# A one-core decoder layer: every second score block of group 0 copied out of PSUM by ScalarE and masked by GpSimd

## What is computed

```python
q = (q @ fq1_w.T + fq1_b) * (q @ fq2_w.T + fq2_b)      # 16 heads of 16 features
k = (k @ fk1_w.T + fk1_b) * (k @ fk2_w.T + fk2_b)
# chunks of 64 tokens: masked scores inside a chunk, a running sum k^T v before it
s = jnp.where(tril, qc @ kc.T, 0.0)
o = inter + s @ vc                                      # linear: no softmax
o = o * rsqrt(mean(o * o, -1) + EPS) * norm_w
x = layernorm(x + o @ wo.T)
```

## Time and profile before

| | us |
| --- | --- |
| median of 3 runs | 573.58 |
| lowest, highest | 573.35, 573.89 |
| the profiled execution | 574.25 |
| its span | 572.5 |
| busy in the span: PE, DVE, ACT, POOL | 531.6, 381.1, 156.8, 132.2 |

### The profile page before, as it was taken

One profiled execution on the slowest core, in us unless ns is written; L12 is line 12 of the kernel. 1 busy time (PEld: TensorE's weight loads), 2 busy tenths in 40 slices (PEclk: granted clock), 3 DMA queues, 4 the chain that ended last, 5 costly groups with the idle time before them and its releaser, 6 DMA issues.

```text
span 572.5 us, 8538 instructions
## 1 busy us (share of the span) xinstructions
PE 531.6 (93%) x3152; PEld 426.0 (74%) x3152; DVE 381.1 (67%) x814; ACT 156.8 (27%) x291; POOL 132.2 (23%) x195
## 2 busy tenths in 40 slices
PE   5975699799999999999999999999999999899994
PEld 5734587646887888765888888765888888688883
DVE  4597589877689976875455666875455677823234
ACT  3433101443323222242222112152222111223330
POOL 2020384110005433121004333121004451200001
PEclk9996699989999999999999999999999999999998
DMA  7423231311114110032001110031002110000001
GB/s 204 126 52 82 74 92 56 97 46 26 37 38 131 43 40 9 1 96 91 1 0 60 37 43 10 0 95 55 1 1 56 47 48 0 32 6 2 1 0 37
DMA packets 25257, 26.80 MB, mean 47 GB/s; under 512 B 2816, under 2 KB 22784, under 8 KB 25216
## 3 DMA queue, kind: packets, MB, share of 16 engines
q1 hardware_dynamic: 14208, 15.73, 9.5%
q10 hardware_dynamic: 10576, 8.95, 5.2%
q0 software_dynamic: 432, 1.57, 0.8%
HBM read 24.15 MB, written 2.10 MB: 46 GB/s over the span
## 4 chain that ended last, share of the span: by engine, by line
PE 79%; DVE 12%; issue 3%; ACT 2%; POOL 1%; DMA 1%; ACTq 0%; POOLq 0%; DVEq 0%
PE bank L955 18%; PE bank L957 17%; PE bank L956 17%; PE bank L1002 5%; PE bank L1065 5%; PE bank L1068 5%; PE bank L1066 5%; PE bank L1042 3%; PE bank L1012 2%; DVE qbd L707 2%; DVE weight L664 1%; PE bank L1076 1%; DMA wo_sb<-in_woT 1%; PE bank L1024 1%; DVE ffn_lo L671 1%
## 5 line engine op out<-in xcount | busy, mean ns | idle before, releaser
L955 PE MATMUL bank<-x2T_lo,ffn_hi 128*128 128x512 f32 x256 | 110.9, 433 | 5.0 <-DVE x2T_lo L833 2.9
L906 DVE TENSOR_TENSOR inter<-bank,inter 128x512 f32<-128x512 f32 x64 | 44.2, 690 | 99.7 <-PE bank L957 99.7
L957 PE MATMUL bank<-x2T_hi,ffn_hi 128*128 128x512 f32 x256 | 102.0, 398 | 0.0
L956 PE MATMUL bank<-x2T_hi,ffn_lo 128*128 128x512 f32 x256 | 101.4, 396 | 0.0
L446 POOL TENSOR_TENSOR qbd<-qT_sb,ctxT_sb 128x256 f32<-128x256 f32 x128 | 79.8, 647 | 85.0 <-PE bank L1068 68.7
L955 PE MATMUL bank<-ffn_lo,inter_hi 128*128 128x256 f32 x256 | 77.8, 304 | 1.3 <-DVE inter_lo L900 1.0
L396 POOL TENSOR_TENSOR ve<-ve,minus_half 128x2 f32<-128x2 f32 x24 | 16.8, 716 | 266.7 <-DVE ve L757 198.3
L605 ACT ACTIVATE inter_hi<-inter 128x512 fp32r<-128x512 f32 x64 | 40.4, 632 | 129.4 <-DVE inter L906 129.4
L957 PE MATMUL bank<-ffn_hi,inter_hi 128*128 128x256 f32 x256 | 72.5, 283 | 0.0
L956 PE MATMUL bank<-ffn_hi,inter_lo 128*128 128x256 f32 x256 | 72.4, 283 | 0.0
L599 ACT ACTIVATE inter<-bank 128x512 f32<-128x512 f32 x64 | 38.1, 595 | 124.9 <-PE bank L957 124.9
(11 more groups left out here) (118 smaller groups left out, 793.8 us busy)
## 6 DMA issues: line engine op xcount, KB each, us to landing
toep_sb<-in_toep ACTq DMA_DIRECT2D x64, 128.0 KB, 2.1
xT_sb<-in_xT SPq DMA_DIRECT2D x4, 512.0 KB, 5.4
ctxT_sb<-in_ctxT SPq DMA_DIRECT2D x4, 512.0 KB, 4.7
x_sb<-in_x SPq DMA_DIRECT2D x4, 512.0 KB, 5.8
ctx_sb<-in_ctx SPq DMA_DIRECT2D x4, 512.0 KB, 6.5
out<-ctxT_sb POOLq DMA_DIRECT2D x3, 512.0 KB, 3.4
raw_w<-in_gate_p SPq DMA_DIRECT2D x8, 128.0 KB, 2.3
raw_s<-in_gate_s SPq DMA_DIRECT2D x8, 128.0 KB
```

The lines of the kernel that those rows point to most:

```text
L906: nc.vector.tensor_tensor(inter[:, n % 2, :], up_ps[:, :], inter[:, n % 2, :], ALU.mult).then_inc(inter_ready, 1)
L955: nc.tensor.matmul(ps, w_hi, x_lo, start=start, stop=False, skip_group_check=True)
L956: nc.tensor.matmul(ps, w_lo, x_hi, start=False, stop=False, skip_group_check=True)
L957: return nc.tensor.matmul(ps, w_hi, x_hi, start=False, stop=stop, skip_group_check=True)
```

## The change

In group 0 the blocks v = 1, 3, 5 and 7 no longer go through DVE. ACT copies each of their two banks into `sc_sb[1]`, and POOL sets the part above the diagonal to zero there with one `affine_select` over 128 x 1024 elements. PE's waits are split to match: the banks of an odd block are free when ACT has copied them, and O(v) of an odd v waits for POOL. In ACT's and POOL's queues the new work stands ahead of the spread of v + 2 that the same call issues (on POOL for odd v; on ACT the spreads belong to even v). Groups 1 to 3 do the same work as before, with the counts of the waits adjusted.

```diff
+        def copied(g, v):
+            return g == 0 and v % 2 == 1 and v < 8
@@ gpsimd: score(g, v)
+                if copied(g, v):
+                    pool.wait_ge(sraw_ready, 2 * (v // 2 + 1))
+                    rows = sc_sb[v % 2].rearrange("p n h c -> p (n h) c")
+                    nc.gpsimd.affine_select(out=rows, in_=rows, compare_op=ALU.is_ge, fill=0.0, base=0,
+                                            pattern=[[0, HT], [1, P]], channel_multiplier=-1)\
+                        .then_inc(sp_ready, 1)
                 if v + 2 < 8 and v % 2:
                     spread(g, v + 2)
@@ scalar: score(g, v)
+                if copied(g, v):
+                    count(act, s_mm, 8, g, v + 1)
+                    count(act, o_mm, 8, g, v - 1)
+                    for r in range(2):
+                        nc.scalar.activation(sc_sb[v % 2][:, r].rearrange("p h c -> p (h c)"),
+                                             score_ps(g, v)[r][:, :], ACT.Copy).then_inc(sraw_ready, 1)
                 if v + 2 < 8 and v % 2 == 0:
                     spread(g, v + 2)
@@ vector: score(g, v)
-                if v == 8:
+                if v == 8 or copied(g, v):
                     return
@@ tensor
+            def masked(g, v):
+                if g == 0 and v % 2:
+                    pe.wait_ge(sp_ready, v // 2 + 1)
+                elif g == 0:
+                    pe.wait_ge(sm_ready, v + 2)
+                else:
+                    count(pe, sm_ready, 16, g, 2 * v - 6)
@@ tensor: score(g, v), before the scores of v
-                    count(pe, sm_ready, 16, g, 2 * (v - 1 if g == 0 else v))
+                    if g:
+                        masked(g, v - 1)
+                    elif v >= 2 and copied(0, v - 2):
+                        pe.wait_ge(sraw_ready, 2 * (v // 2))
+                    elif v >= 2:
+                        masked(0, v - 2)
@@ tensor: score(g, v), before the output of v - 1
-                    count(pe, sm_ready, 16, g, 2 * v + 2)
+                    masked(g, v)
@@ tensor: sums(g, mt)
-                count(pe, sm_ready, 16, g, 14 if g == 0 else 16)
+                masked(g, 6 if g == 0 else 7)
```

More of the change, by code:

```diff
@@ L178, in decoder_layer @@
             "filled", "const_ready", "pool_mask", "kv_ready", "prod_ready")
-        last_mm, last_stored = sems("last_mm", "last_stored")
+        last_mm, last_stored, sraw_ready, sp_ready = sems("last_mm", "last_stored", "sraw_ready", "sp_ready")
         rstd_ready = sems("rstd_ready1", "rstd_ready2", "rstd_ready3")
```

## The result

The changed kernel takes 576.09 us (median of 19 runs, 573.87 to 579.56), the kernel before 573.63 us in the same comparison (19 runs). The ratio is 1.0037 with a 95% interval of 1.0023 to 1.005, so the change costs 1.3 to 2.9 us, 2.1 by the ratio itself. (The two medians lie 2.46 us apart; the verdicts here go by the ratio.) Timed again beside other kernels the ratio was 1.0028, interval 1.0016 to 1.004. The forecast was 575.6, slower by 2.0.

What follows compares the result with a forecast made beforehand. DVE was taken to bound group 0's score stage, 4.47 us for two blocks. A POOL loop of 4.88 us put `sums(1)` 1.84 us later; with 0.2 for contention, 573.58 + 2.0 = 575.6 us, range 574.0 to 578.6.

Steps and rivals of the forecast that it cites:

- What bounds: Group 0's score stage: DVE is full with masks and unpack, 4.47 us for two blocks against PE's 3.26.
- where the shift goes: End of group 0's score stage: the later start of `sums(1)` carries to the kernel's end one for one, +2.0 us.
- the walk: Score stage followed event by event from S0 at 26.67 to `sums(1)` at 47.92 us, 1.84 later than before.
- The loop: Odd blocks: S(v), ACT copies, POOL select, then the spread queued behind it, which S(v + 2) awaits; 4.88 us.
- The select: POOL's select of 128 x 1024 in each odd block, taken as 1.3 us between bounds of 1.03 and 2.35.
- Two of POOL's 0.12: SBUF contention in the score stage: two POOL operations on the path each 0.12 us longer, counted as 0.2 us.
- DVE's 0.85: Score stage: DVE's loss when L671 meets a spread (1.53 for 0.68 us), taken as hidden by 1.6 us slack.
- third rival: Dearer POOL work in the score stage, by element cost or DVE operations coming first; +1.8 to 4.2 us on top, 19%.
- DVE's idle time: Score stage: the 4.8 us taken from DVE become idle time ahead of even masks, some 1 to 2 us a lap.
- first rival's point of decision: DVE relief wins in the score stage if each of four selects is 0.8 us shorter than taken; 6%.
- The clock: PE's granted clock stays 1.00 through the score stage to about 46 us; a fall, up to +2.6 us, had 8%.
- parts named for "slower": Whole kernel: chance of being slower by more than 0.2%, given as 0.72, summed from shares of the forecast and its rivals.

Runs made afterwards that it cites:

- e1: Changed kernel with POOL's spread of v + 2 put ahead of the select of v; ratio to the kernel before 0.9999, stage 19.54 us.
- e4: Changed kernel with the score stage's four weight units moved to group 0's convolution; stage 19.69 us, whole 587.01 us in one run, only the stage is read.
- e2: Changed kernel with the select over one head, 128 x 128, the other seven left unmasked (work left out); ratio to the kernel before 0.9972.
- e5: Kernel before plus a POOL select of 128 x 1024 after the spreads of 3, 5 and 7 that nobody waits for; ratio 1.0069.
- e3: Changed kernel with only block 7 copied by ACT and masked by POOL, blocks 1, 3 and 5 through DVE as before; ratio to the kernel before 0.9984.

## Why the prediction was right, point by point

**What bounds, and where the shift goes.** That the stage was DVE's was right. That the shift of its end carries to the end of the kernel one for one agrees with the ratios and is not shown more closely: `outproj` starts 3.02 us later (57.92 for 54.90), at 205.70 us the shift is 2.27 in one execution and 0.44 in the other, and the forecast had 2.0 at both places. The times of events were close, measured from S0. The forecast column is the walk, without the 0.2 us for contention; with it `sums(1)` stood at 48.1, which is 21.4 from S0.

| | forecast | measured |
| --- | --- | --- |
| S3 | 6.08 | 5.73 |
| S5 | 10.96 | 10.73 |
| S7 | 15.84 | 15.74 |
| O7 | 19.72 | 19.79 |
| `sums(1)` | 21.25 | 21.26 |

**The loop.** The named mechanism, the spread behind the select, is shown by e1: turning these two round takes 1.72 of the stage's 1.85 us away. It is half of the cause: with the queue as it was and the unpack away (e4), 1.57 of them go too. The lap came out at 5.00 for a forecast of 4.88.

**The select was mis-sized, with the right sum.** I took 1.30 us; with nothing in its way it is 1.09, close to the 1.12 that POOL's two-input rows gave and far from 1.75 and 2.35. Beside DVE it is 1.57. Four of them are 1.09 + 3 x 1.57 = 5.80, and I had 5.2 and 0.2 for contention. The difference of 0.4 was more than paid by hops that were shorter than I took them: ACT to POOL 0.07 for 0.15, the spread's end to PE 0.05 for 0.14, PE to ACT 1.18 for 1.23. So errors in both directions met, and it is luck that +1.85 agrees with +2.0 better than the terms do. That the profiled execution, at 576.46, came so close to the forecast's 576.25 is luck as well, since +1.13 and -0.8 us of it come from outside the stage.

**Contention was the failed step.** "Two of POOL's 0.12" stood for it. That figure was one meeting in which POOL had started first, and so hardly waited; DVE's 0.85 was the waiting side. In this loop the select starts 0.07 us behind L687 each time, since both are counted from the end of the same spread: it releases S3 and with it the copy and the select, and it ends DVE's L697 and with it the mask, L680 and L687. So POOL is the one that waits, for what is left of L687. By the Trainium skill (SBUF — State Buffer, Who interferes with whom) the port pair that the two engines share is an exclusive lock, and issue order decides who is blocked. The trace agrees, 1.57 us for 1.09, and e2 and e4 show it: the same 0.48 or 0.49 us on 128 elements as on 1024, and none with the units moved. This was the third rival's mechanism, at 0.48 us in three selects; what I had as 0.68 in each lap. It was the forecast's and the rival's at once, and they should not have been set against each other.

**DVE's idle time did not come.** I expected 1 to 2 us of idle DVE in each lap. The view of busy time shows 4.00 of 4, since the two L697 count as busy while they wait for POOL. In the changed kernel that costs nothing further: O3 waits for the select (0.45 us of idle PE ahead of it), not for mask 2; the 0.77 us that PE waits for mask 2 ahead of O2 are over well before. In e5, where DVE is the bound, the same waiting costs 0.9 us and more a lap.

**The first rival's point of decision** was right in kind. With the select 0.79 us shorter (0.78 for 1.57) e2 is faster than before. So the sign of this change hung on the length of one POOL instruction, as the sum had it. **The clock** held to 1.00 up to 46 us in the changed kernel, as forecast; e5 shows that a wait of 2.83 us in this stage was followed by the lower level.

**What wasn't forecast** is what the surroundings add to a single execution: +1.13 and -0.8 us in the profiled one. The first is the landing of `wo_sb`, long before the stage. It took 6.3 us in the kernel before and 6.9 to 7.95 in the changed kernel and its variants; with one profiled execution of the kernel before it stays open whether the kernel has a part in that. Whether the earlier rise of the clock in `outproj` follows from the later start of the stage stays open: it was 6.13 us before, 5.59 and 5.30 in two executions of the changed kernel, but 6.32 in e1 and 6.67 in e3. The recorded chances hold one small slip: the parts named for "slower" add up to 0.73, not 0.72.

## What to carry to other kernels

When work is moved to an engine with idle time, look first at what stands behind it in that engine's queue and is waited for by another: here 4.8 us taken from the full engine were worth nothing, because a spread that PE needs was put behind a select that it doesn't need yet, and because that select waited for DVE. Taking either away brought the kernel or its stage back to about where it was before; of the two, only both together made the stage shorter than before. Price a GpSimd operation beside VectorE by who starts first: with the unpack's operations here the second waited for the rest of the first, and the wait was booked as busy time of the waiting engine. A forecast that comes out right should still be taken apart into its terms; here a select taken too long by 0.2 us in each of four places and a contention too small by 1.2 us in sum hid each other.

## What the runs showed of the hardware

- A select of 128 x 1024 fp32 on POOL takes 1.09 us and one of 128 x 128 0.29: 0.89 ns per element and 0.18 us fixed.
- POOL's select and spread and some of DVE's operations hold each other up. L687 (two SBUF inputs) went from 0.68 to 1.57 us beside a select (e1), L697 (TENSOR_SCALAR of 128 x 256 int32) from 0.28 to 1.18 beside a select and to 1.12 beside a spread, and a select from 1.09 to 1.57 behind L687. The masks, which read PSUM and one SBUF tile, stayed at 1.28 for two beside a spread (before, and e1).
- Between two POOL operations that followed each other at once, one DVE operation came through: an L697 ended 0.15 us after the select did, the next one 0.15 us after the spread.
- ACT's L513 beside the start of a select cost the select nothing: 1.09 us (changed kernel, first lap).
- Hops measured in the loop of the changed kernel: ACT's end to POOL's start 0.07 us, the spread's end to PE's start 0.05, the select's end to PE's start 0.15.
